# Attention scores in half-width matmuls, with the relative position bias in unused rows; constants and gate steps placed anew

## The reference, cut to what matters

```python
xn = layernorm(xc, ln1_scale, ln1_bias)              # over the 64 channels
qkv = windows(xn) @ w_qkv + b_qkv
attn = einsum('bnhd,bmhd->bhnm', q * scale, k)       # 64 x 64 for each window and head
attn = attn + rel_bias_table[REL_IDX]                # one 64 x 64 table for each head
attn = softmax(attn)
xc = xc + (attn @ v) @ w_proj + b_proj
xc = xc + gelu(layernorm(xc) @ w_mlp1 + b_mlp1) @ w_mlp2 + b_mlp2
...
h = relu(pw1(x)); scores = sigmoid(fc2(relu(fc1(mean(pw1(x))))))
mask = top 32 of the 64 scores; offsets = tanh(off_w(mean(h)))
w = base * (1 + sigmoid(offset0)) + tanh(offset1)    # 3x3, 5x5, 7x7 depthwise, own weights for each image
out = pw(concat of the three convolutions) + x
```

## Time and profile before

| | us |
|---|---|
| median of three runs | 355.97 (354.71 to 358.31) |
| the profiled execution, whole | 358.61 |
| its span, first to last instruction | 356.8 |
| mean granted TensorE clock | 0.978 |

### The profile page before, as it was taken

How to read it: one execution, slowest core, us unless ns; L and a number is a source line. 1 busy time by engine, 2 the same in 40 slices (tenths; PEclk the granted TensorE clock), 3 DMA queues, 4 the chain that set the end, 5 groups by cost and what they waited for, 6 DMA issues and landing times.

```text
span 356.8 us, 6320 instructions
## 1 busy us (share of the span) xinstructions
PE 327.7 (92%) x2442; PEld 225.5 (63%) x2442; DVE 232.1 (65%) x403; ACT 206.1 (58%) x349; POOL 63.6 (18%) x58
## 2 busy tenths in 40 slices
PE   2668899999999999999998999699799899999994
PEld 2344675776767767677677765344367577777773
DVE  6566148188485693875847644578999989667411
ACT  6352835747568476585554468797891674445600
POOL 5461101211213212132011070122220000000000
PEclk9986999999999999999999999999999899999998
DMA  7533272322322133212232000058002665779721
GB/s 179 127 66 74 79 137 60 70 45 57 68 57 54 44 69 67 56 51 61 58 75 56 24 2 2 0 119 188 0 3 57 125 131 120 150 149 182 156 55 29
DMA packets 31148, 27.66 MB, mean 78 GB/s; under 512 B 21008, under 2 KB 27664, under 8 KB 31120
## 3 DMA queue, kind: packets, MB, share of 16 engines
q1 hardware_dynamic: 30544, 26.48, 35.3%
q10 hardware_dynamic: 576, 0.79, 0.9%
HBM read 3.78 MB, written 2.10 MB: 16 GB/s over the span
## 4 chain that ended last, share of the span: by engine, by line
PE 73%; DVE 12%; ACT 7%; DMA 3%; SPq 2%; issue 2%; POOL 1%; DVEq 0%; ACTq 0%
PE psum L1014 19%; PE psum L781 12%; PE psum L797 5%; PE psum L762 4%; PE psum L713 4%; PE psum L806 4%; PE psum L783 4%; PE psum L784 4%; PE psum L763 4%; PE psum L928 3%; DVE maxima L1123 3%; PE psum L740 2%; DMA probs<-in_rel_table 2%; PE psum L814 2%; PE psum L940 2%
## 5 line engine op out<-in xcount | busy, mean ns | idle before, releaser
L1014 PE MATMUL psum<-shifted,conv_w 128*128 128x512 f32 x336 | 87.9, 424 | 0.0
L1014 PEld LDWEIGHTS psum<-shifted,conv_w 128*128 128x128 f32 x336 | 65.0, 194 | 21.8 <-issue 1.3
L543 ACT ACTIVATE probs<-psum 128x512 f32<-128x512 f32 x64 | 38.3, 599 | 50.2 <-PE psum L784 49.3
L781 PE MATMUL psum<-q_heads,k_blocks 128*128 128x512 f32 x192 | 59.7, 419 | 0.0
L1123 DVE TENSOR_REDUCE maxima<-psum 128x8 f32<-128x512 f32 x64 | 41.2, 685 | 23.9 <-PE psum L763 23.9
L781 PEld LDWEIGHTS psum<-q_heads,k_blocks 128*128 128x128 f32 x192 | 35.0, 189 | 14.2 <-issue 7.7
L285 POOL TENSOR_TENSOR parts<-x,parts 128x256 fp32r<-128x256 f32 (+1 forms) x21 | 19.1, 922 | 101.8 <-ACT parts L492 56.9
L762 PE MATMUL psum<-k_heads,q_blocks 128*128 128x512 f32 x64 | 27.8, 434 | 4.0 <-DMA k_heads<-k_parts 3.4
L713 PE MATMUL psum<-parts,center_average 128*128 128x512 f32 x64 | 22.4, 434 | 9.6 <-DVE parts L285 7.9
L1137 DVE RECIPROCAL inv_sum<-psum 128x256 f32<-128x256 f32 x16 | 28.0, 1750 | 3.3 <-PE psum L806 3.2
L271 ACT CAST conv_w<-conv_w 32x896 fp32r<-32x896 f32 x31 | 29.1, 938 | 0.4
(11 more groups left out here) (142 smaller groups left out, 506.3 us busy)
## 6 DMA issues: line engine op xcount, KB each, us to landing
shifted<-images SPq DMA_DIRECT2D x32, 332.5 KB, 5.5
k_blocks<-k_parts SPq DMA_DIRECT2D x32, 128.0 KB, 2.8
q_heads<-q_parts SPq DMA_DIRECT2D x128, 32.0 KB, 1.9
k_heads<-k_parts SPq DMA_DIRECT2D x64, 32.0 KB, 1.8
out<-x SPq DMA_DIRECT2D x8, 256.0 KB, 5.5
x<-in_x SPq DMA_DIRECT2D x6, 256.0 KB, 5.0
x<-in_x SPq DMA_DIRECT2D x4, 128.0 KB, 4.4
weights<-in_weights ACTq DMA_DIRECT2D x1, 443.0 KB, 7.6
```

Source lines behind the costliest of these rows:

```text
L543: act.activation(probs[:, w, :], psum[:, PROB0 + w % 2, :], ACT.Exp).then_inc(S["ac_probs"], 1)
L781: pe.matmul(bank, k_blocks[:, w // (NW // 2), k_part, w % (NW // 2), :], q_heads[:, q_part, :, w * T:(w + 1) * T], start=k_part + q_part = ...
L1014: ins = pe.matmul(psum[:, CONV0 + bh, :], conv_w[bh][:, w_part, t, :], img[:, y:y + H - 1:2, x0:x0 + W], start=t == 0 and w_part + part == ...
```

## The change

Heads 0 to 3 of queries and keys now lie in partitions 0 to 63 (image half 0 in the first 32, image half 1 in the next), heads 4 to 7 in 64 to 127; the host lays the weights and biases out for it. A matmul for four heads (256 columns) so uses 64 of 128 rows, and the other 64 carry the bias: `reverse` on the side of the blocks, the bias on the side of the heads. The maximum pass has two matmuls of 256 columns in place of two of 512. Scores have one of 512 (`pick`) and six of 256 in place of five of 512. The bias in the maximum pass is its high part alone.

- The blocks' unused rows are set once: `q_blocks` by VectorE (`query_constants`), `k_blocks` by ScalarE (high part) and GpSimd's memset (low part), `k_heads` by VectorE (`bias_with_keys`), `q_heads` by VectorE for windows 0 to 3 (`bias_with_queries`) and by ScalarE for windows 4 to 7. The memsets of `k_heads`, `q_heads` and `q_blocks` go.
- ScalarE fills `q_blocks` in two steps of two copies (`block_queries`): half 0 behind `evacuate_q`, half 1 in the next step behind exponential 4. A copy has 32 rows, not 64. `high_of_x` goes ahead of `evacuate_k`.
- SyncE: queries half 0, then all four key-block DMAs after the scores of the whole group, then queries half 1.
- The last variance uses bank 2 and waits for the last projection's evacuation, not for gelu; `mlp1(3)` no longer waits for its logarithm, `pointwise1(1)` does.
- Gates: `low_even(0, 0)` goes behind `gate_hidden(1)`, `gate_hidden(2)` ahead of `result(0, 0)`, and TensorE's `gate_spread(2)` behind all of `high_passes(1, 0)`.

```diff
+    "not_in_half": (_p // 64)[:, None] != np.arange(2),
-        k_blocks = at("k_blocks", [128, 2, 2, NW // 2, 2 * T], F32R)
+        k_blocks = at("k_blocks", [128, 2, 2, 2, NW // 2, 2 * T], F32R)
-        q_blocks = at("q_blocks", [128, NW, 2 * T], F32R)
+        q_blocks = at("q_blocks", [128, 2, NW, 2 * T], F32R)
-        VAR2_LAST = 6
+        VAR2_LAST = 2
+        def bias_rows(rel, half, windows):
+            rel = of_half(rel.bitcast(F32).rearrange("p (h t) -> p h t", h=NH), half)
+            return rel.unsqueeze(2).to_broadcast([128, NH // 2, len(windows), T])
...
+            def spread_key_blocks(n):
...
+                    sp.wait_ge(S["pe_scores"], NW * n)
+                sp.wait_ge(S["dv_k_low"], n + 1)
+                for hh in range(2):
+                    for bh in range(2):
+                        r = slice(hh * 64 + bh * 32, hh * 64 + bh * 32 + 32)
+                        sp.dma_start(k_blocks[r, hh, ...], k_parts[r, n % 2]).then_inc(S["k_blocks_in"], 16)
...
             for g in range(NG - 1):
-                for half in range(2):
-                    spread_parts(g + 1, half)
+                spread_queries(g + 1, 0)
+                spread_key_blocks(g + 1)
+                spread_queries(g + 1, 1)
...
+            def block_queries(half, par):
                 for bh in range(2):
-                    r = slice(bh * C, (bh + 1) * C)
+                    r = slice(half * 64 + bh * 32, half * 64 + bh * 32 + 32)
...
                 exponentials(g, 4)
+                if nxt is not None:
+                    block_queries(1, 1 - par)
...
             square_of_centered(0)
+            for half in range(2):
+                ins = act.activation(k_blocks[:, half, :, 0], reversal()..., ACT.Copy, scale=not_in_half(half))
...
             square_of_centered(1)
+            for part, rel in enumerate((rel_high, rel_low)):
+                for half in range(2):
+                    ins = act.activation(query_rows(part, half, late), bias_rows(rel, half, late), ACT.Copy, scale=not_in_half(half))
...
-                    pe.wait_ge(S["q_blocked"], n + 1)
+                    pe.wait_ge(S["q_blocked"], 2 * (n + 1))
...
-                pe.matmul(max_bank(w), q_blocks[:, w, :], k_heads[:, :, w * T:(w + 1) * T], start=True, stop=False)
-                pe.matmul(max_bank(w), reverse[:], rel[:, 0, :], start=False, stop=True).then_inc(S["pe_max"], 1)
+                for hh in range(2):
+                    ins = pe.matmul(max_bank(w)[:, hh * G // 2:(hh + 1) * G // 2], q_blocks[:, hh, w, :],
+                                    of_half(k_heads, hh)[:, :, w * T:(w + 1) * T], start=True, stop=True)
+                ins.then_inc(S["pe_max"], 1)
...
+                pe.matmul(bank, pick[:, w, :], minus_max[:, :, :], start=True, stop=False)
+                for hh in range(2):
+                    for k_part, q_part in ((0, 0), (0, 1), (1, 0)):
+                        ins = pe.matmul(bank[:, hh * G // 2:(hh + 1) * G // 2], k_blocks[:, hh, w // (NW // 2), k_part, w % (NW // 2), :],
+                                        of_half(q_heads[:, q_part], hh)[:, :, w * T:(w + 1) * T], start=False, stop=hh + k_part == 2)
...
-                    pe.wait_ge(S["ac_gelu"], 12)
+                    pe.wait_ge(S["ac_proj"], NG)
...
-            high_passes(1, 0, range(0, TAP))
+            high_passes(1, 0)
             gate_spread(2)
-            high_passes(1, 0, range(TAP, NKT))
...
-            split_bias()
+            query_constants()
+            high_of_bias(0, rel_flipped, "dv_rel_flipped")
             normalise(0)
+            bias_with_keys()
             k_low(0, 0)
+            high_of_bias(1, rel_high, "dv_rel_high")
             q_low(0, 0)
+            low_of_bias()
+            bias_with_queries()
             other_weights()
...
             whole_weights(1, 0)
+            gate_hidden(2)
             result(0, 0)
             low_weights(1, 0)
-            gate_hidden(2)
```

More of the change, by code:

```diff
@@ L304, in halves, with patches, of_half, not_in_half @@
             return t.rearrange("p (s c) -> p s c", s=2)
-        ZERO_Q_BLOCKS, ZERO_Q_HEADS, NZERO, NBORDER = 1, 4, 5, 3
+        NZERO, NBORDER = 2, 3
+        def patches(n):
+            return rel_raw[:, n, :, :].rearrange("p (a b) h -> p h a b", a=WS)[:, :, :, 0:WS]
+        def of_half(t, half):
+            return t[:, half * (NH // 2):(half + 1) * (NH // 2), :]
+        def not_in_half(half):
+            a = _AT["not_in_half"][0] + half
+            return consts[:, a:a + 1]
+        def reversal():
+            return const("reverse").unsqueeze(1).to_broadcast([128, NW, 128])
+        def bias_rows(rel, half, windows):
+            rel = of_half(rel.bitcast(F32).rearrange("p (h t) -> p h t", h=NH), half)
+            return rel.unsqueeze(2).to_broadcast([128, NH // 2, len(windows), T])
+        def key_rows(half):
+            return of_half(k_heads, half).rearrange("p h (w t) -> p h w t", t=T)
+        def query_rows(part, half, windows):
+            rows = of_half(q_heads[:, part], half).rearrange("p h (w t) -> p h w t", t=T)
+            return rows[:, :, windows.start:windows.stop, :]
         block = ctx.enter_context(nc.Block())
@@ L402, in _ @@
         def _(pool):
-            for t in (q_blocks[:].bitcast(F32), k_blocks[:].bitcast(F32), gaps[:]):
-                pool.memset(t, 0.0).then_inc(S["zeroed"], 1)
+            pool.memset(k_blocks[:, :, :, 1].bitcast(F32).rearrange("p h s w t -> p (h s) (w t)"), 0.0).then_inc(S["k_blocks_zeroed"], 1)
+            pool.memset(gaps[:], 0.0).then_inc(S["zeroed"], 1)
             pool.wait_ge(S["consts_in"], 16)
@@ L588, in step @@
                     inverse_deviation2(prev)
+                if after is not None:
+                    high_of_x(after)
                 if far is not None:
@@ L591, in step @@
                     evacuate_q(far, par)
-                if after is not None:
-                    high_of_x(after)
             square_of_centered(0)
             act.dma_start(weights[:, _WAT["vec"][1]:], d["weights"][:, _WAT["vec"][1]:]).then_inc(S["weights_in"], 16)
+            act.wait_ge(S["consts_in"], 16)
+            for half in range(2):
+                ins = act.activation(k_blocks[:, half, :, 0], reversal().rearrange("p (s w) t -> p s w t", s=2), ACT.Copy, scale=not_in_half(half))
+            ins.then_inc(S["k_blocks_set"], 1)
             inverse_deviation(0)
@@ L602, in _ @@
             evacuate_q(0, 0)
+            block_queries(1, 0)
             act.wait_ge(S["v_zeroed"], 1)
@@ new lines, in bias_with_keys, with bias_with_queries @@
+            def bias_with_keys():
+                for half in range(2):
+                    ins = dve.tensor_scalar(key_rows(half), bias_rows(rel_flipped, half, range(NW)), not_in_half(half), None, ALU.mult)
+                ins.then_inc(S["k_heads_set"], 1)
+            def bias_with_queries():
+                early = range(NW // 2)
+                for part, rel in enumerate((rel_high, rel_low)):
+                    dve.wait_ge(S["dv_rel_low" if part else "dv_rel_high"], 1)
+                    for half in range(2):
+                        ins = dve.tensor_scalar(query_rows(part, half, early), bias_rows(rel, half, early), not_in_half(half), None, ALU.mult)
+                ins.then_inc(S["q_heads_set0"], 1)
@@ new lines, in high_of_bias, with low_of_bias @@
+            def high_of_bias(n, rel, done):
+                dve.wait_ge(S[f"rel_in{n}"], 16)
+                for half in range(2):
+                    ins = dve.tensor_copy(rel[half * T:(half + 1) * T].rearrange("p (h a b) -> p h a b", h=NH, a=WS), patches(n))
+                ins.then_inc(S[done], 1)
+                dve.wait_ge(S[done], 1)
+            def low_of_bias():
+                for half in range(2):
+                    r = slice(half * T, (half + 1) * T)
+                    high, low = (t.rearrange("p (h a b) -> p h a b", h=NH, a=WS) for t in (rel_high[0:T].bitcast(F32), rel_low[r]))
+                    ins = dve.tensor_tensor(low, patches(1), high, ALU.subtract)
+                ins.then_inc(S["dv_rel_low"], 1)
```

99 lines of the change are left out of this document (44 added, 55 removed).

## The result

| | before | after |
|---|---|---|
| median | 357.14 us (4 runs, 354.71 to 359.16) | 345.24 us (4 runs, 343.12 to 346.23) |
| ratio | | 0.965, 95% interval 0.9602 to 0.9699 |
| profiled execution, its span | 358.61, 356.8 | 343.12, 341.3 |

The kernel is faster, by 11.9 us. The forecast was 16.7 us less and 339. The time lies inside the range of 332 to 348, but outside the 335 to 343 of the forecast itself; it falls where rival C was put, 343 to 347.

A forecast was written before the change was run, and what follows sets the result against it. TensorE, busy 92% of 356.8 us, was taken as the bound, with chains of VectorE, ScalarE and GpSimd close behind. Loop 11.7, start 1.0, after the loop 0.5, convolution 3.5 sum to 16.7 off 355.97: 339 us, range 332 to 348.

The forecast's parts named there:

- rival C: Loop as forecast, but start at its high bound (+4) and a wait left at third gate (+3.5): 343 to 347; chance 0.17.
- The matmul price: Attention loop: a 256-column matmul with its weight load costs 0.12 us, saving TensorE alone 3.4 us a step.
- Rival B: Weight loads not hidden behind 256 columns, a pair costs 0.19 to 0.23 us: 360 at 0.19; chance 0.07.
- Not 3.4 but some 1.5 us a step: Full loop step: gains 0.3 and 1.5 in its halves, less 0.3 for restarts; bounds 0.8 to 2.0.
- First half: Loop step from scores of window 0 to the first maximum pass: -0.3 us, new query copies covered on TensorE.
- A: Loop: TensorE stays the only bound and the whole 3.4 us a step counts, 325.6; chance 0.06.
- D: Loop: TensorE's new waits drop its clock once a step, 1.7 us a time, 13.6 in all, 353; chance 0.05.
- The loop: Eight attention steps: steps 0 to 6 gain 1.5 us each, step 7 gains 1.2, together -11.7.
- SyncE's queue: Loop's key and query DMAs: 13.4 us after scores 7, priced at nothing; comes back if a step falls under 20.5.
- The start: Before the loop: VectorE's constants at the low price of 8 us, first scores at 35.5 instead of 36.55, -1.0.
- After the loop: Between loop and convolution: last variance no longer waits for gelu, -0.5 us; moving low_even counted 0.
- The third gate: Convolution: wait for gate_hidden(2) goes, -1.8 us, and the half clock following it, -1.7; together -3.5.

The follow-up runs named there:

- Experiment 8: Kernel after with the second query copies moved from behind exponential 4 to directly behind evacuate_q, all four together: 343.88 us, ratio 0.9618, step 21.34.
- experiment 9: Kernel after with the low part of the far square on VectorE instead of GpSimd: 341.11 us, ratio 0.9536, step 21.16.
- experiment 5: Kernel after without the product of the keys' low part with the queries' high part, sixteen half-width pairs a step fewer: 344.26 us, ratio 0.9621, step 21.32.
- the repeat: Kernel after run again without any edit, for a second profile and more times: 344.86 us, ratio 0.9629.
- experiment 12: Kernel after with experiment 11's two edits, and VectorE's other_weights moved behind the first group's spread_maxima: 340.0 us, ratio 0.9513.
- experiment 7: Kernel after with each VectorE maximum taken over 16 of the 64 keys of a window and head: 341.62 us, ratio 0.9553, step 21.44.
- experiment 11: Kernel after with all query copies behind evacuate_q and the far square's low part on VectorE: 340.04 us, ratio 0.9529, step 20.70.
- experiment 2: Kernel before with only the three moves of gate steps (low_even, result and low_weights behind gate_hidden): 353.57 us, ratio 0.9868.
- experiment 4: Kernel before with only the last variance moved to bank 2 and its waits changed: 356.29 us, ratio 0.9943.
- experiment 10: Kernel before with the low part of the far square on VectorE instead of GpSimd: 357.35 us, ratio 1.0002, step 23.09.
- experiment 3: Kernel after with the three gate steps put back in their old places: 348.11 us, ratio 0.9717.
- experiment 6: Kernel before without the product of the keys' low part with the queries' high part, one full-width matmul a window: 348.78 us, ratio 0.9757, step 22.08.

## Why the prediction was right or wrong

**The matmul price: right.** 0.118 us a pair, 0.12 forecast. Rival B, the side of slower, needed 0.1725 and falls. The Trainium skill's rule weighed there ("TensorE: Matmul & The Clock Gate", Part 3, what overlaps) doesn't hold for these loads: full-height loads of 128 columns hide behind 256-column matmuls, at 0.118 us a pair. The prediction's estimate from the page's figure for a load was some 0.21.

**Not 3.4 but some 1.5 us a step: right in size, wrong in its parts.** The full step is 21.77 us, 21.7 forecast. Second half: forecast -1.5 with +0.3 for restarts, measured -1.41, VectorE without a gap, as said. First half: forecast -0.3, measured 0.

The step of the prediction that failed lies between the variance and the first maximum pass: "weighted values and sums (about 1.9 us) cover the 1.3, with some 0.1 left over", with block 4's -0.20 counted beside it. Up to the variance the half fell by 0.24 us, as forecast. From the variance to the pass it grew from 3.68 to 3.93 us, where the forecast had some 0.1 less. The path there is ScalarE's. From the variance to the end of exponential 4 it is 2.59 us before and 2.61 after, and the copies come behind that. The rows of the kernel before already tell it:

```profile
115.27 1.10 PE L797 MATMUL psum<-probs,v_blocks 128*32 128x64 f32 x64
115.49 0.58 ACT L543 ACTIVATE probs<-psum 128x512 f32<-128x512 f32 x1
...
116.18 1.05 PE L806 MATMUL psum<-probs,consts 128*32 128x256 f32 x16
```

The cover starts at 115.27, the exponential ends at 116.07, so 0.8 of the cover is gone before a copy could start. Two copies of 0.62 would end at 117.31, 0.15 us behind the pass at 117.16. The cheaper block 4 lets the cover start, and end, 0.2 earlier, and doesn't move ScalarE's chain, so its gain turns into waiting. Together that is the 0.36 measured: the sums end at 112.22, the copies at 112.53. The chain starts at the variance, which waits for GpSimd. I had named GpSimd's low parts as late next and didn't follow them through exponential 4 into the copies. Experiment 8 prices the copies at 0.43 a step and experiment 9 the low part at 0.61.

The forecast of the step came out because this error and the restarts, forecast at 0.3 and not seen in the second half, offset each other. That is luck.

**Rivals A and D: both fall.** A needed TensorE to be the only bound: experiment 5 gives back 0.45 of 1.9, so it falls. D, half clock once a step, doesn't show: behind step 0 the loop of the kernel after is at 1.00 with its waits of 0.2 to 0.5. Experiment 5 has a wait of 1.1 us in each of steps 1 to 5, and they too are at 1.00; its two slow stretches lie in step 0.

**Rival C: its number, not its causes.** The measured 345.24 lies in C's 343 to 347. But C needed a late start (+4) and a wait left at the third gate (+3.5). The start came 1.1 us earlier in one profile and 0.3 later in the other, and the wait at the gate is gone. What fills the gap to the forecast is below: the loop, the start, and the clock at the gate.

**The loop: -10.5 in the profile of after, -9.9 in that of the repeat, -11.7 forecast.** Of the 1.2 short, 0.8 is step 0 (22.99; forecast as a full step's gain, got 0.70). Its first half already hung on ScalarE and GpSimd: 47.27 - 35.42 = 11.85 us, against 48.24 - 36.55 = 11.69 before, so only the second half gained. Steps 1 to 5 gave 6.9 of 7.5, steps 6 and 7 gave 2.85 of 2.7 (2.4 in the repeat, where the queue, next, held them up more).

**SyncE's queue: wrong, by the prediction's own sign.** It was priced at nothing, and key heads awaited in the loop were to show the prediction wrong. In steps 1 to 5 nothing waits for it. But k_heads is awaited in step 6 (0.24 us at 176.12) and k_blocks at the start of step 7 (0.52 at 186.76); in the repeat it is 0.71 and 0.55, 1.26 us together. The prediction said that the queue comes back under a step of 20.5 us and didn't apply this to step 6, which has no keys and queries of a further group to make: it is 19.50 us, 20.02 in the repeat. In the faster experiments it came back above 20.5 too: in step 1 of experiments 8, 9 and 12 (0.48, 1.14 and 0.61 us), and in experiment 7 at the start of it (1.51). In experiment 11 the waits are 0.41 and 0.58.

**The start: the steps as forecast, the gain only in part.** VectorE's constants took 8.1 us, the low price, and 6.6 in the repeat:

```profile
8.90 1.41 DVE L1143 TENSOR_SCALAR q_blocks<-consts 128x1024 fp32r<-128x1024 f32 x2
...
12.36 2.94 DVE L1148 TENSOR_SCALAR k_heads<-normed,consts 128x2048 fp32r<-128x2048 f32 x2
...
20.46 3.77 DVE L1156 TENSOR_SCALAR q_heads<-normed,consts 128x1024 fp32r<-128x1024 f32 x4
...
22.08 1.33 PE L813 MATMUL psum<-k_heads,q_blocks 128*128 128x256 f32 x6 [4.59 <-DMA k_heads<-k_parts]
...
25.33 2.47 DVE L1189 TENSOR_REDUCE maxima<-psum 128x8 f32<-128x512 f32 x4
```

The first pass goes 2.2 us earlier than in the earlier trace rows, and the maxima start where they did. But the first scores come at 35.42 in one execution and 36.87 in another of the same kernel, with 36.55 before. Over the profiles here, kernels with the old layout start them at 35.9 to 37.5 and those with the new at 35.1 to 37.5. The two executions of the kernel after part at VectorE's first work on the input. After, and then the repeat:

```profile
4.30 0.50 DVE L1116 CAST parts<-x 128x256 fp32r<-128x256 f32 x2 [1.01 <-DMA x<-in_x]
```

```profile
5.28 0.49 DVE L1116 CAST parts<-x 128x256 fp32r<-128x256 f32 x2 [2.03 <-DMA x<-in_x]
```

So 1.0 of the 1.45 us is the landing of the input, and 1.2 has built up when the maxima start (26.52 against 25.33). In the kernel before this work starts at 5.43, right behind the memset of k_heads, so an earlier landing could have gained little there. With the new layout it starts at 4.3 to 4.7 in four of nine profiles, and the first scores then come at 35.3 to 36.5. In the other five it starts at 5.3 to 5.7, and they come at 36.9 to 37.5, but for experiment 7 with its shorter maxima (35.1).

The rest, 0.26 us, comes behind the maxima and goes with the clock. The window 28 to 32 in after, and then in the repeat:

```profile
28.00:32.00 4.00, 1.50 (x7) 1.00 (x6) 2.87 (x5) 1.67 (x4) 1.40 (x2) 0.84 0.18 56
```

```profile
28.00:32.00 4.00, 2.52 (x10) 2.03 (x9) 2.67 (x5) 1.92 (x4) 1.03 (x2) 0.50 0.16 49
```

In the repeat TensorE is at half clock for 17.1 us unbroken (22.0 to 39.1), in after for 6.8 and 3.4. From the last maximum to the first scores it takes 3.47 us there against 3.21. All nine profiles of the new layout show 10.2 to 17.1 us at half clock in the start, the five of the old one 3.4 to 10.2, and the mean granted clock of the ten runs of the kernel after is 0.969 to 0.983, with 0.977 to 0.995 before. So more time at half clock goes with the change, which the forecast did not have. What that costs in all was not measured. The gain of this part, forecast at 1.0, is not told apart from zero.

**After the loop: 1.03 instead of 0.5.** The bank gave its 0.5. The other 0.55 is low_even behind gate_hidden, priced at 0; experiment 2 shows it alone. On VectorE it had held up the x that the pointwise convolution waits for.

**The third gate: the wait right, the clock too high.** Forecast 1.8 + 1.7, measured 2.8 in the spans of this stage and 3.3 to 3.6 in the medians for the whole of the gate steps, low_even's 0.55 included. The 1.8 is there in every profile with the old order of the gate. The half clock behind it is in those of before and of experiments 4 and 10, and not in those of 3 and 6, so it was a part of the one execution I read, and of three of the five profiles with this wait. Taken as certain, it was mis-sized.

**The sum.** Against the repeat's spans (356.8 - 343.4 = 13.4) the forecast of 16.7 is 3.3 too high: 1.8 too much in the loop, 1.3 in the start (which came 0.3 later there, not 1.0 earlier) and 0.7 in the convolution, less the 0.5 too little after the loop. The 1.1 between 13.4 and the 12.3 of the medians lies with the one execution of before that was profiled (358.61 against a median of 357.14). The range held because it was wide enough for errors of this size, not because each term was right.

## What to carry to other kernels

When an engine is busy for all of a step, take its work away in thought and follow each chain that it hid, one stage further than the first late engine: here GpSimd's low part reached the maximum pass by way of an exponential and two copies. Leaving a product out of the kernel before (experiment 6) would have priced the bound ahead of the change: 1.09 us came off for 1.84 removed. A limit worked out for the full step has to be held against the short steps too: SyncE's queue was fast enough for 21.77 us and not for 19.50. A stretch at half clock in a single profile is to be priced by how often it comes: here it stood behind the same wait in three profiles of five.

## What the runs showed of the hardware

- The same kernel gets a different clock in the same place: 17.1 us at half clock from 22.0 in one execution, 6.8 and 3.4 us in another. An idle stretch of TensorE of 1.74 to 1.77 us was followed by 3.4 us at half clock in three kernels' profiles and by none in two others'.
- A copy on ScalarE of 32 rows by 512 elements takes 616 ns a piece (L566, below), one of 64 rows took 617: half the rows took the same time, so four copies of 32 rows in place of two of 64 doubled the copies' time (19.7 us against 9.9).

```profile
L566 ACT CAST q_blocks<-q_parts 32x512 fp32r<-32x512 f32 x32 | 19.7, 616 | 0.6
```

- A 128x128 weight load in front of each 256-column matmul was hidden: the pairs came 0.118 us apart, half of the 0.23 us of a 512-column one.
